# Cross-attention in a gated decoder: turned probabilities copied in pairs of units, attention outputs in one PSUM bank

## What is computed

```python
q = _w8a8_linear(x, wq, bq)            # 16 heads of 32 channels
k = cond @ wk.T + bk;  v = cond @ wv.T + bv
scores = einsum('bhnd,bhld->bhnl', q, k) / sqrt(32) + mask[:, None]
attn = softmax(scores, axis=-1)
o = einsum('bhnl,bhld->bhnd', attn, v)
x = x + tanh(g) * _w8a8_linear(o, wo, bo)
x = x + tanh(g2) * bitlinear_ffn(layernorm(x))
```

## Time and profile before

| | |
|---|---|
| median of three runs | 1027.84 us |
| the profiled execution | 1027.91 us, its span 1026.1 us |
| mean granted TensorE clock | 0.959 of full speed |
| TensorE matmuls busy | 899.2 us (88%) |
| VectorE busy | 699.0 us (68%) |
| ScalarE busy | 540.0 us (53%) |
| exp, L1191 | 256 of 693 ns |
| mask and maximum, L1674 | 256 of 703 ns |
| copies of turned probabilities, L1700 and L1182 | 128 of 686 ns, 128 of 588 ns |
| output copy, L1197; output scaling, L1714 | 32 of 396 ns, 32 of 417 ns |

### The profile page before, as it was taken

One profiled execution on the slowest core, in us unless ns is written; L12 is line 12 of the kernel. 1 busy time (PEld: TensorE's weight loads), 2 busy tenths in 40 slices (PEclk: granted clock), 3 DMA queues, 4 the chain that ended last, 5 costly groups with the idle time before them and its releaser, 6 DMA issues.

```text
span 1026.1 us, 15751 instructions
## 1 busy us (share of the span) xinstructions
PE 899.2 (88%) x5584; PEld 589.6 (57%) x5592; DVE 699.0 (68%) x1890; ACT 540.0 (53%) x1072; POOL 71.5 (7%) x73
## 2 busy tenths in 40 slices
PE   3989999999997973799898899898899898899567
PEld 2878767676774642566444576443566444567233
DVE  5995872424220684799786799786799787899564
ACT  4546211111110672689446689456688547688243
POOL 2000222121200000000100000100000010000100
PEclk9989999999999987899999999998999999999779
DMA  6435642121200958600179300178200179200001
GB/s 196 141 135 164 210 150 72 56 69 55 70 1 21 353 162 159 165 4 2 42 157 174 116 7 1 43 152 179 88 34 2 42 141 188 83 1 2 1 1 42
DMA packets 49581, 94.43 MB, mean 92 GB/s; under 512 B 8284, under 2 KB 8284, under 8 KB 48480
## 3 DMA queue, kind: packets, MB, share of 16 engines
q1 hardware_dynamic: 43584, 82.37, 30.1%
q0 software_dynamic: 3136, 10.52, 3.0%
q10 hardware_dynamic: 2784, 0.54, 0.4%
HBM read 47.23 MB, written 14.75 MB: 60 GB/s over the span
## 4 chain that ended last, share of the span: by engine, by line
PE 35%; DVE 10%; SPq 7%; issue 6%; ACT 5%; DMA 4%; POOL 0%; POOLq 0%; DVEq 0%; ACTq 0%
PE psum L1390 7%; PE psum L1407 6%; PE psum L1365 6%; SPq L1041 6%; PE psum L1463 5%; PE psum L1433 5%; DMA k<-k_lo 4%; ACT probs L1191 2%; PE psum L1332 1%; PE psum L1449 1%; DVE amax L1612 1%; SPq L1052 1%; DVE xn L1780 1%; PE psum L1416 1%; DVE stats L1775 1%
## 5 line engine op out<-in xcount | busy, mean ns | idle before, releaser
L1191 ACT ACTIVATE probs<-psum,neg_max 128x512 f32<-128x512 f32 x256 | 175.0, 693 | 32.3 <-DVE neg_max L1674 32.1
L1674 DVE CUSTOM_DVE_ANT_0 psum<-psum,m_in 128x512 f32<-128x512 f32 x256 | 174.0, 703 | 18.1 <-issue 18.1
L1390 PE MATMUL psum<-ident,probs 128*128 128x128 f32 x1024 | 153.8, 274 | 0.0
L1390 PEld LDWEIGHTS psum<-ident,probs 128*128 128x128 f32 x1024 | 127.3, 141 | 20.5 <-issue 3.3
L1365 PE MATMUL psum<-k,q 128*128 128x512 f32 x256 | 125.6, 496 | 13.6 <-ACT probs L1191 7.9
L568 PE MATMUL psum<-w_sb,hT 128*128 128x512 f32 x256 | 114.4, 592 | 0.0
L465 ACT ACTIVATE hT<-psum,b_col 128x256 f32<-128x256 f32 x64 | 26.9, 471 | 153.6 <-PE psum L490 153.5
L1700 DVE COPY probsT<-psum 128x512 f32<-128x512 f32 x128 | 87.7, 686 | 2.8 <-PE psum L1390 2.5
L1182 ACT COPY probsT<-psum 128x512 f32<-128x512 f32 x128 | 75.2, 588 | 19.3 <-PE psum L1390 19.3
L488 PE MATMUL psum<-xselT_hi,w_hi 128*128 128x256 f32 x256 | 81.6, 319 | 1.6 <-ACT xselT_hi L459 1.6
L1365 PEld LDWEIGHTS psum<-k,q 128*128 128x128 f32 x256 | 48.9, 191 | 50.0 <-ACT probs L1191 32.9
(11 more groups left out here) (212 smaller groups left out, 1541.6 us busy)
## 6 DMA issues: line engine op xcount, KB each, us to landing
c_in<-in_ctx_dram SPq DMA_DIRECT2D x8, 1024.0 KB, 5.6
bw_in<-in_L_ffn_W_dram SPq DMA_DIRECT2D x8, 1024.0 KB, 12.3
k<-k_hi SPq DMA_DIRECT2D x32, 256.0 KB, 6.4
k<-k_lo SPq DMA_DIRECT2D x32, 256.0 KB, 7.6
q<-q_hi SPq DMA_DIRECT2D x64, 128.0 KB, 3.5
q<-q_lo SPq DMA_DIRECT2D x64, 128.0 KB, 3.5
xres<-in_x_dram SPq DMA_DIRECT2D x4, 1024.0 KB, 6.3
w_raw<-in_L_ffn_w_dram POOLq DMA_DIRECT2D x4, 1024.0 KB, 5.5
```

Source lines behind the costliest of these rows:

```text
L1191: act.activation(probs[:, u % 4, :], psum[u % SCORE_BANKS][:, :], ACT.Exp, scale=-1.0, bias=neg_max[:, u:u + 1], accum_out=prob_sum[:, nt, ...
L1390: mm = pe.transpose(turn_bank(u)[:, l * P:(l + 1) * P], probs[:, u % 4, l * P:(l + 1) * P], ident[:, :])
L1674: dve.tensor_tensor_reduce(bank[:, :], bank[:, :], m_in[:, nt, :], -1.0, LOWEST, ALU.add, ALU.min, neg_max[:, u:u + 1]).then_inc(masked_re ...
```

## The change

The eight PSUM banks become one tensor, `sh.banks`, so that one access pattern can span two banks. There are four turn banks now (3 to 6), used as two pairs; unit u goes to bank 3 + u % 4. A pair of units (2m, 2m + 1: one head, two token tiles) is copied by one instruction of 1024 elements per partition (`turned_pair`, `pair_home`): VectorE at u % 4 == 1, ScalarE at u % 4 == 3. The semaphores count one for each pair, and TensorE waits for a pair's copy before the first unit of the pair that uses the same two banks. All attention outputs go to one bank, `psum[7]`. The output is copied by ScalarE at step 5 of its half group, turned by TensorE at step 6 and scaled by VectorE at step 7; the reciprocals are at step 5. The value matmuls of a half group wait for the scaling of the one before it (`o_ready`, from hg = 1 on). A wait for `x_done` is added at unit 2, whose turn bank follows a bank that the feed-forward block used. The loop has three steps fewer at its end.

```diff
--- before.py
+++ after.py
@@ -112,7 +112,8 @@
         sh.w_amax = sb("w_amax", [P, 2, C // P])
         sh.w_scale = sb("w_scale", [P, 2, C // P])
         sh.w_inv = sb("w_inv", [P, 2, C // P])
-        sh.psum = [ctx.enter_context(nc.psum_tensor(f"psum{i}", [P, 512], F32)) for i in range(8)]
+        sh.banks = ctx.enter_context(nc.psum_tensor("banks", [P, 8 * 512], F32))
+        sh.psum = [sh.banks[:, 512 * i:512 * (i + 1)] for i in range(8)]
         sh.psum_b = [t[:, :].bitcast(BF16) for t in sh.psum]
         sh.psum_i = [t[:, :].bitcast(I16) for t in sh.psum]
         sh.x_mid = [nc.dram_tensor(f"x_mid{b}_dram", (x.shape[1], C), F32, kind="Internal").ap() for b in range(x.shape[0])]
@@ -971,24 +972,34 @@
         out_stored = sem("out_stored")
 
         LAG = 3
-        SCORE_BANKS, TURN_BANKS = 3, 3
+        SCORE_BANKS, PAIR_UNITS = 3, UNITS // 4
         HALF = 2 * P
         HG = 2 * GROUPS
         UH = UNITS // HG
         STACKS = HPG * 4
         AV_STEPS = 4
 
-        STEPS = UNITS + LAG + UH + 3
+        STEPS = UNITS + LAG + UH
 
         CONTEXT_BANKS = (0, 1, 2, 4)
 
+        AV_BANK = psum[7]
+
         def turn_bank(u):
-            return psum[SCORE_BANKS + u % TURN_BANKS]
-
-        def past_half_group(s, delay):
-
-            hg, i = divmod(s - LAG - UH - delay - UH + 1, UH)
-            return hg if 0 <= hg < HG and i == 0 else None
+            return psum[SCORE_BANKS + u % 4]
+
+        def turned_pair(m):
+            first = SCORE_BANKS + 2 * (m % 2)
+            return sh.banks[:, 512 * first:512 * (first + 2)].rearrange("p (u l n) -> p u l n", u=2, l=T)
+
+        def pair_home(m):
+            hg, r, nt = unit(2 * m)
+            return probsT[:, (hg + 1) % 2, r, :, :].rearrange("p l (u n) -> p u l n", u=2)
+
+        def within_half_group(s, step):
+
+            hg, i = divmod(s - LAG - UH, UH)
+            return hg if 0 <= hg < HG and i == step else None
 
         def unit(u):
 
@@ -1172,15 +1183,14 @@
                         if more and s == UNITS + LAG + 1:
                             turned_context(b + 1)
                         u = s - LAG
-                        if 0 <= u < UNITS and u % 2 == 1:
+                        if 0 <= u < UNITS and u % 4 == 3:
                             hg, r, nt = unit(u)
                             if hg == 1:
                                 act.wait_ge(q_stacked[1], b * 16 * STACKS + 16 * STACKS)
                             if hg >= 2:
                                 act.wait_ge(av_psum, b * HG + hg - 1)
                             act.wait_ge(pT_psum, b * UNITS + u + 1)
-                            act.copy(probsT[:, (hg + 1) % 2, r, :, (nt % 2) * P:(nt % 2) * P + P],
-                                     turn_bank(u)[:, :].rearrange("p (l n) -> p l n", l=T)).then_inc(pT_ready[1], 1)
+                            act.copy(pair_home(u // 2), turned_pair(u // 2)).then_inc(pT_ready[1], 1)
                         if s < UNITS:
                             u = s
                             hg, r, nt = unit(u)
@@ -1191,10 +1201,10 @@
                             act.activation(probs[:, u % 4, :], psum[u % SCORE_BANKS][:, :], ACT.Exp, scale=-1.0,
                                            bias=neg_max[:, u:u + 1],
                                            accum_out=prob_sum[:, nt, h:h + 1]).then_inc(probs_ready, 1)
-                        hg = past_half_group(s, 1)
+                        hg = within_half_group(s, 5)
                         if hg is not None:
                             act.wait_ge(av_psum, b * HG + hg + 1)
-                            act.copy(attnT[:, hg % 2, :], psum[6 + hg % 2][:, 0:HALF]).then_inc(av_ready, 1)
+                            act.copy(attnT[:, hg % 2, :], AV_BANK[:, 0:HALF]).then_inc(av_ready, 1)
 
                 def hidden(b, t):
                     for f in range(FQ):
@@ -1383,9 +1393,10 @@
                         u = s - LAG
                         if 0 <= u < UNITS:
                             pe.wait_ge(probs_ready, b * UNITS + u + 1)
-                            if u >= TURN_BANKS:
-                                v = u - TURN_BANKS
-                                pe.wait_ge(pT_ready[v % 2], b * (UNITS // 2) + v // 2 + 1)
+                            if u == 2:
+                                pe.wait_ge(x_done, b * T + 1)
+                            if u >= 4 and u % 2 == 0:
+                                pe.wait_ge(pT_ready[u // 2 % 2], b * PAIR_UNITS + u // 4)
                             for l in range(T):
                                 mm = pe.transpose(turn_bank(u)[:, l * P:(l + 1) * P], probs[:, u % 4, l * P:(l + 1) * P], ident[:, :])
                             mm.then_inc(pT_psum, 1)
@@ -1394,26 +1405,26 @@
                         if 0 <= hg < HG and i % AV_STEPS == 0:
                             if i == 0:
                                 for k in range(2):
-                                    pe.wait_ge(pT_ready[k], b * (UNITS // 2) + (hg + 1) * UH // 2)
+                                    pe.wait_ge(pT_ready[k], b * PAIR_UNITS + (hg + 1) * UH // 4)
                                 if more and hg == HG - 1:
                                     context(b + 1, c_in)
-                                if hg >= 2:
-                                    pe.wait_ge(o_ready, b * HG + hg - 1)
+                                if hg >= 1:
+                                    pe.wait_ge(o_ready, b * HG + hg)
                                 else:
                                     pe.wait_ge(x_done, b * T + 1)
                             for l in range(T * i // UH, T * (i + AV_STEPS) // UH):
                                 for r in range(HPG):
                                     h = (hg // 2) * HPG + r
-                                    mm = pe.matmul(psum[6 + hg % 2][HD * r:HD * (r + 1), 0:HALF],
+                                    mm = pe.matmul(AV_BANK[HD * r:HD * (r + 1), 0:HALF],
                                                    vv[:, l, h * HD:(h + 1) * HD],
                                                    probsT[:, (hg + 1) % 2, r, l, :], start=(l == 0), stop=(l == T - 1))
                             if l == T - 1:
                                 mm.then_inc(av_psum, 1)
-                        hg = past_half_group(s, 3)
+                        hg = within_half_group(s, 6)
                         if hg is not None:
                             pe.wait_ge(av_ready, b * HG + hg + 1)
                             for k in range(2):
-                                mm = pe.transpose(psum[6 + hg % 2][:, HALF + k * P:HALF + (k + 1) * P],
+                                mm = pe.transpose(AV_BANK[:, HALF + k * P:HALF + (k + 1) * P],
                                                   attnT[:, hg % 2, k * P:(k + 1) * P], ident[:, :])
                             mm.then_inc(o_psum, 1)
 
@@ -1690,30 +1701,29 @@
                             dve.scalar_tensor_tensor(xres[:, t, :], bo_row[:, :], gate_x1, x_in[:, t, :],
                                                      ALU.mult, ALU.add).then_inc(x_used, 1)
                         u = s - LAG
-                        if 0 <= u < UNITS and u % 2 == 0:
+                        if 0 <= u < UNITS and u % 4 == 1:
                             hg, r, nt = unit(u)
                             if hg == 1:
                                 dve.wait_ge(q_stacked[1], b * 16 * STACKS + 16 * STACKS)
                             if hg >= 2:
                                 dve.wait_ge(av_psum, b * HG + hg - 1)
                             dve.wait_ge(pT_psum, b * UNITS + u + 1)
-                            dve.tensor_copy(probsT[:, (hg + 1) % 2, r, :, (nt % 2) * P:(nt % 2) * P + P],
-                                            turn_bank(u)[:, :].rearrange("p (l n) -> p l n", l=T)).then_inc(pT_ready[0], 1)
-                        hg = past_half_group(s, 2)
+                            dve.tensor_copy(pair_home(u // 2), turned_pair(u // 2)).then_inc(pT_ready[0], 1)
+                        hg = within_half_group(s, 5)
                         if hg is not None:
                             g, n0 = hg // 2, 2 * (hg % 2)
                             dve.wait_ge(probs_ready, b * UNITS + (hg + 1) * UH)
                             dve.reciprocal(prob_inv[:, n0:n0 + 2, g * HPG:(g + 1) * HPG],
                                            prob_sum[:, n0:n0 + 2, g * HPG:(g + 1) * HPG]).then_inc(link.sem, 1)
                             link.count += 1
-                        hg = past_half_group(s, 3)
+                        hg = within_half_group(s, 7)
                         if hg is not None:
                             g, n0 = hg // 2, 2 * (hg % 2)
                             link.wait()
                             dve.wait_ge(o_psum, b * HG + hg + 1)
                             dve.tensor_tensor(
                                 xn[:, n0:n0 + 2, g * P:(g + 1) * P].rearrange("p t (r d) -> p t r d", r=HPG),
```

(2 more changed lines are left out.)

## The result

The changed kernel takes 1076.99 us, median of four runs (1073.37 to 1080.43), against 1027.21 for the kernel before: ratio 1.0484, 95% interval 1.0454 to 1.0513. The forecast was 1077.4. The profiled execution took 1079.22 us with a span of 1077.1, 51.0 more than before. It is one of the two longer executions: the mean granted clock of TensorE was 0.956 in those two (1079.22 and 1080.43 us) and 0.964 and 0.960 in the other two (1074.76 and 1073.37 us).

A forecast was written before the change was run, and what follows sets the result against it. The prediction took a closed chain through ScalarE and TensorE, 8.76 us per half group, as the bound. Periods 43.0, filling 0.2 and tails 6.4 sum to 49.6 more than 1027.8: 1077.4 us, range 1041 to 1090.

The forecast's parts named there:

- The loop of 8.76: In attention before the change: a closed chain of waits through ScalarE and TensorE, 8.76 us per half group.
- Prices of the copies: Pair copies on VectorE and ScalarE: 1.22 and 1.01 us long, holding their queues for 1.17 and 0.91 us.
- The hand-over: Attention output at steps 5 to 7: TensorE waits at the output transposes for ScalarE's copy, about 1 us a period.
- the walk: Working through one half group's operations leg by leg with the new lengths and order until the state repeats: 10.55 us.
- The period: One half group in steady attention of the changed kernel: 10.55 us, 1.79 more than 8.76.
- fourteen legs: The start-to-start times along the new closed chain of one half group, 0.25 to 1.17 us each, sum 10.55 us.
- Filling and tails: Start and end of each attention stretch: filling 0.04 us more, tail 1.6 us more, in four batch elements 0.2 and 6.4.
- The clock: TensorE's granted clock in attention: stays at 2.4 GHz (1.00), with TensorE near 80% busy in the new period.
- nothing changed between the attention stretches: Sign of a right forecast: the parts of the kernel between attention stretches stay as before.
- Rival C: TensorE's clock falls to 1.2 GHz in attention: 67 us more, 1144 us; chance 0.02.
- Rival A: Only the output's hand-over costs: period about 9.2 us, 24 x 0.4 and part of the tail, 1041 us; chance 0.13.
- Rival B: At step 6 ScalarE has copied the output before TensorE arrives, so no queue is held: 22 us less, 1006; chance 0.09.

The follow-up runs named there:

- f1: The kernel before, with only the value matmuls moved one step later (steps 1 and 5 instead of 0 and 4): 1013.1 us, ratio 0.9868.
- e2: The changed kernel with each pair copy made as two single copies one behind the other at the same place: 1078.1 us, ratio 1.0499 to the kernel before.
- e3: The changed kernel, pairs kept, with ScalarE's output copy ahead of the exp of step 4: 1061.8 us, ratio 1.0349 to the kernel before.
- e1: The changed kernel with single alternating copies instead of pairs, its banks and hand-over kept: 1051.9 us, ratio 1.0249 to the kernel before.
- p1: The changed kernel with value matmuls and hand-over one step later and the output copy ahead of the exp of step 6: 1018.5 us, ratio 0.9930.

## Why the prediction was right

- *What bounds the kernel before:* right. The loop of 8.76 was a closed chain through ScalarE and TensorE; f1 opened it and gained 0.63 a period.
- *Prices of the copies:* right. 1.22 us and 1.007 us long, 1.15 and 0.89 in the queue, taken as 1.17 and 0.91. The Trainium skill's 186 + 0.833 ns per element ("ScalarE: Activation LUTs", What ACT_TABLE_LOAD costs) gives an estimate of 1039 ns; the rows of this kernel gave 1010 and were nearer to the 1007 measured.
- *The hand-over:* right, in place and size. TensorE's weight load waits 0.90 us at the transposes; the walk had 0.96.
- *The period:* 10.41 for 10.55; fourteen legs, none off by more than 0.05 but more of them too long than too short, 24 x 0.14 = 3.4 us in the sum.
- *Filling and tails:* 0.04 and 1.6 each; measured -0.1 (14.72 us for 14.86 in the last batch element) and 1.7.
- *The clock:* right for the steady periods (1.00), and "nothing changed between the attention stretches" held in the sum and not in each place (up to 2.8 us); wrong for the ends of three stretches, where it fell to 1.2 GHz and cost 4.5 us. Rival C looked only at the mean over a period, and the sum had no term for the ends. What makes the clock fall there stays open. The Trainium skill ("TensorE: Matmul & The Clock Gate", Part 1) has the clock taken back when TensorE idles. The trace agrees only in part: the falls came behind idle pieces of at most 1.2 us, at three of four ends, and the same pieces brought none at the first end, in e2 and in e3.
- So the closeness of 1077.4 is in part luck: 3.4 us too much in the periods, 4.5 too little for the clock in the profiled execution, and a median that lies 2.2 us below that execution.
- *Rival A* (1041, hand-over alone): e1 has that kernel at 1051.9, so the hand-over costs more than the rival's 0.4 us a period. Walked leg by leg, as it was for e1 (9.8), it would have been priced nearly right. *Rival B* (faster): p1 shows that its condition can be met, by other places for the same instructions. The rival named the right point, step 6, but took one wait for the only one; e3 shows the second behind it.

## What to carry to other kernels

When three in-order engines hand one another short work, write down the chain that closes on itself, leg by leg, and check that its sum is the measured period; then put a change's new lengths and new order into it. Merging two operations into one saves one overhead (0.20 us a period between e2 and the changed kernel), and costs its whole length to everything that stands behind it, so look first at what follows it in the queue and whether another engine waits for that. A consumer that is released by the step just before it is the first thing to move: one step later was worth 1.3% here, two steps nothing.

## What the runs showed of the hardware that was not expected

TensorE's granted clock fell in the changed kernel at the end of three of four attention stretches, for some four microseconds (0.50 to 0.57; context transposes 3.48 us instead of 1.94), after some 2.2 us of idle time in pieces of 0.3 to 1.2 us with transposes in between. The first stretch, and the profiled executions of e2 and e3, have the same pieces (within 0.1 us) and kept it at full speed.

One copy over two PSUM banks costs no more than its elements: 1220 ns on VectorE and 1007 on ScalarE for 1024, against 686 and 588 for 512 in one bank, and 1.28 and 1.07 us for two in a row in e2.
